# Four products of a constant in every step of TensorE's loop in the nodes stage

## The reference, cut to what matters

```
x = x + graph(layernorm(x)) + mix(layernorm(x))     # x1
u = layernorm(x)
logits = u @ gate_w + gate_b; idx = argmax(softmax(logits))
pos = running count of the rows of each expert; kept = pos < 977
y = relu(u_e @ w1[e] + b1[e]) @ w2[e] + b2[e]       # for the kept rows of expert e
x = x + y * prob
```

## Time and profile before

| what | value |
|---|---|
| median of three runs | 2139.8 us (2136.44 to 2140.73) |
| the profiled execution | 2139.9 us, span 2138.3 us |
| mean granted clock of TensorE | 0.787 of 2.4 GHz |
| nodes stage in the span | about 1544 to 1671 us |
| busy in the span | PE 1593.7, DVE 1387.2, POOL 1036.1, ACT 721.3 us |

### The profile page before, as it was taken

One profiled execution on the slowest core, in us unless ns is written; L12 is line 12 of the kernel. 1 busy time (PEld: TensorE's weight loads), 2 busy tenths in 40 slices (PEclk: granted clock), 3 DMA queues, 4 the chain that ended last, 5 costly groups with the idle time before them and its releaser, 6 DMA issues. The chain is left out here.

```text
span 2138.3 us, 26245 instructions
## 1 busy us (share of the span) xinstructions
PE 1593.7 (75%) x6551; PEld 889.5 (42%) x6551; DVE 1387.2 (65%) x4056; ACT 721.3 (34%) x2020; POOL 1036.1 (48%) x1021
## 2 busy tenths in 40 slices
PE   4666887677878777365555658888676699999997
PEld 3552332233333333022222224554365466666665
DVE  7568998789999998366656555555465144444444
ACT  3336997004877776000000001111064122222221
POOL 2001001777777777777777777777425111111111
PEclk9788999767999999555555557667555799999999
DMA  5117000333333333933333344444844422222200
GB/s 167 40 40 295 31 0 15 100 101 96 94 97 97 99 97 99 99 110 103 103 101 103 102 114 130 123 121 128 102 155 168 133 89 89 97 92 92 91 23 5
DMA packets 89183, 210.70 MB, mean 99 GB/s; under 512 B 20627, under 2 KB 49849, under 8 KB 86081
## 3 DMA queue, kind: packets, MB, share of 16 engines
q0 software_dynamic: 51888, 138.08, 24.8%
q1 hardware_dynamic: 35496, 70.56, 9.7%
q10 hardware_dynamic: 1680, 0.67, 0.2%
HBM read 163.98 MB, written 49.89 MB: 100 GB/s over the span
## 5 line engine op out<-in xcount | busy, mean ns | idle before, releaser
L902 DVE TENSOR_TENSOR XA<-XA,bank 128x257 f32 x880 | 369.0, 419 | 345.0 <-PE bank L657 319.5
L439 POOL DMA_INDIRECT G<-xn_parts,idx x440 | 443.0, 1007 | 277.7 <-DVE srcl L994 143.9
L439 POOL DMA_INDIRECT w<-xn_parts,idx x440 | 451.3, 1026 | 134.1 <-issue 134.1
L656 PE MATMUL bank<-G,S 128*128 128x257 f16 x440 | 154.8, 352 | 165.2 <-DMA G<-xn_parts,idx 140.4
L1582 POOL DMA_INDIRECT out<-ob,tok x64 | 66.6, 1040 | 401.7 <-DVE ob L1568 399.0
L656 PE MATMUL bank<-w,S 128*128 128x257 f16 x440 | 152.6, 347 | 138.8 <-DMA w<-xn_parts,idx 124.0
L529 ACT ACTIVATE LV<-LH,v 125x128 f16<-125x128 f16 x600 | 182.9, 388 | 189.5 <-DVE LH L1063 189.2
L1506 PE MATMUL bank<-w,ht 128*117 128x256 f32 (+1 forms) x1024 | 223.7, 379 | 0.0
L1495 PE MATMUL bank<-xt,w 128*128 128x468 f32 (+1 forms) x512 | 215.3, 579 | 0.8 <-ACT xt L1520 0.8
L1506 PEld LDWEIGHTS bank<-w,ht 128*117 128x117 f32 (+1 forms) x1024 | 188.8, 186 | 30.5 <-issue 0.4
L1530 ACT ACTIVATE ht<-bank,b1c 128x468 f32<-128x468 f32 (+1 forms) x128 | 85.7, 670 | 333.8 <-PE bank L1495 333.8
(11 more groups left out here) (225 smaller groups left out, 2542.9 us busy)
## 6 DMA issues: line engine op xcount, KB each, us to landing
w<-f SPq DMA_DIRECT2D x16, 1024.0 KB, 7.4
expert_rows<-G SPq DMA_DIRECT2D x7, 2048.0 KB, 21.3
xb<-expert_rows SPq DMA_DIRECT2D x8, 1028.0 KB, 11.4
xb<-expert_rows SPq DMA_DIRECT2D x8, 939.7 KB
G<-xn_parts,idx POOLq DMA_INDIRECT x440, 2.8
w<-xn_parts,idx POOLq DMA_INDIRECT x440, 2.8
XA<-x SPq DMA_DIRECT2D x6, 1024.0 KB, 5.7
xn_parts<-G POOLq DMA_DIRECT2D x12, 512.0 KB, 3.7
```

Source lines behind the costliest of these rows:

```text
L439: pool.indirect_dma_start(g[:, o:o + 2 * D], None, tab, bass.IndirectOffsetOnAxis(ap=idx[:, t:t + 1], axis=0)).then_inc(s_g[t % RING], 16)
L656: pe.matmul(psA[t % AR][:, 0:AGW], lhs, g[:, o + D:o + 2 * D + 1], start=True, stop=True)
L902: v.tensor_tensor(XA[:, ds(o, AGW)], XA[:, ds(o, AGW)], psA[t % AR][:, 0:AGW], ALU.add).then_inc(s_ev, 1)
```

## The change

At the head of each of the 66 steps of TensorE's loop in `nodes` it multiplies a constant (the tile of ones, read as 16-bit numbers) by itself four times, 128x128 by 128x256, into PSUM bank 0, which nobody reads. That is 264 products. In the first 49 steps a wait stands ahead of them: TensorE waits until DVE has finished x1 of block n. Nothing else changes.

```diff
@@ nodes
     PT, PD = 64, 128
+    FILL = 4
...
     @block.tensor
     def _(pe):
+        idle = ones[:, :].bitcast(F16)
         for n in range(STEPS):
+            if n < NB:
+                pe.wait_ge(s_x1, n + 1)
+            for _ in range(FILL):
+                pe.matmul(bank[0][:, 0:2 * P], idle[:, 0:P], idle[:, 0:2 * P], start=True, stop=True)
             m = blk(n, GATE)
```

## The result

| | before | after |
|---|---|---|
| median | 2139.45 us (2136.44 to 2140.73) | 2164.71 us (2155.68 to 2167.45) |
| ratio to before, with its 95% interval | | 1.0111 [1.0089, 1.0132] |
| the profiled execution | 2139.9 us | 2163.4 us, span 2161.8 us |
| mean granted clock | 0.787 | 0.800 |
| PE busy in the span | 1593.7 us, 6551 instructions | 1618.7 us, 6815 instructions |

The account below looks back on a forecast made before the run. The prediction took a ring of TensorE's transposes and ACT's copy and normalising, no engine full, to bound `nodes`. Terms -0.8 + 5.0 + 18.7 + 10.7 - 1.5 = +32.1 on 2139.9 gave 2172.0 us, range 2153 to 2179.

Parts of the forecast that it names:

- L8 to L15: `nodes`, line 1376 of step 8 to that of step 15: full clock, shorter steps, 0.8 us faster.
- L15 to L22: `nodes`, line 1376 of step 15 to step 22: a 19.85 us batch at clock 0.50, less 0.8; 5.0 us slower.
- L22 to L43: `nodes`, line 1376 of step 22 to step 43: three batches of 19.85 us against 13.62, 18.7 us slower.
- L43 to the last places: `nodes` tail, line 1376 of step 43 to the end of L1364: 44.3 us against 33.57, 10.7 us slower.
- hidden by POOL: End of `nodes`: POOL's last batch begins about 0.8 us after the places, before 2.26; saves 1.5 us.
- TensorE's own step at clock 0.50: Undisturbed steps of `nodes`: transposes 0.46, 0.83 to the next work, products 0.85; 2.14 us, more than the old 1.65.
- rival 2: `nodes`: the clock comes and goes, one or two of four batches at 1.00; 2152 to 2167 us, chance 0.22.
- rival 1: `nodes`: the full clock holds through the stage, batches of 15.03 us; about +3, 2143 us, chance 0.08.
- Rival 3: `nodes`: the clock never rises, the constant or too few products not lifting it; +37.6, 2177 us, chance 0.20.
- Rival 4: `nodes`, start of each step: full clock holds, wait costs nothing as line 1376 runs ahead; 2128 us, chance 0.03.
- Rival 5: `nodes`: the products pass beside everything or fall away, no difference; 2140 us, chance 0.02.
- one ring: `nodes`: the wait closes a loop through TensorE, ACT and DVE's line 1376; 19.85 us a batch at 0.50, against 13.62.

Follow-up runs that it names:

- the wait at the full clock: Against the changed kernel: products set by schedule (5, 11 or 9 a step, none in the tail), from step 9 the wait behind them; 2143.29 us, 1.0020 of before.

## Why the prediction was right, and where it was off

**The sum, term by term** (us, from the starts of line 1376 and the last places in the two traces):

| stretch | forecast | measured | how |
|---|---|---|---|
| L8 to L15 | -0.8 | -0.6 | 10.53 against 11.15 |
| L15 to L22 | +5.0 | +4.05 | 18.08 against 14.03 |
| L22 to L43 | +18.7 | +15.5 | 19.10 + 18.13 + 19.11 against 40.86 |
| L43 to the last places | +10.7 | +7.8 | 41.41 against 33.57 |
| hidden by POOL | -1.5 | -1.5 | 0.80 against 2.26 |
| sum | +32.1 | +25.3 | |

The mechanism held in each stretch, and each of the long ones was made too dear: by a fifth to a quarter up to L43, by over a third in the tail. The 0.3 us between the +25.3 of the sum and the 25.0 in the trace is the way from POOL's last batch to `experts`. **The term that was mis-sized is TensorE's own step at clock 0.50**, put at 2.14 us and measured at 1.95. I had added the transposes (0.46), the time from the logits to the next transposes (0.83) and the products (0.85) as if they followed each other; measured are 0.43 for transposes to logits, 0.71 for logits to products and 0.81 for products to transposes. The 0.83 of the earlier trace rows was read in the one step of a batch that has the prefix sums: the logits behind them take 0.98 us and not 0.86, and what follows starts 0.83 after them and not 0.71. The changed kernel has the same 0.83 there, though its next work is the products (they start at 1650.00):

```profile
1649.17 0.98 PE L1293 MATMUL bank<-gw,ut 128*128 128x8 f32 x4
```

So 0.12 us that belong to one step were put into every step. That is 0.12 of the 0.19, and 0.04 and 0.03 are in the other two. Three such steps in a batch are 3 x 0.19 = 0.57 of the 0.75 us by which a batch at 0.50 was too long (19.85 against 19.10). The other hops were good: 1.36 for line 1376 to the transposes (forecast 1.35), 3.21 from transposes to the exponential's reader (3.26), 1.47 to the prefix sums' reader (1.52), 3.50 to the next batch (3.54). Counted with their signs, they make the rest. In the tail the same error stands in every step to T57, which came 31.8 us after L43 (33.7 forecast); and from the last prefix sums to the last places, with the clock at 1.00, it took 3.82 us where 4.31 were put. One slip of the working, 4.87 for L1320 where its terms give 4.85, bears on nothing. And the square roots of steps 8 and 15 have no table load ahead of them (the trace before has its first in the stage at 1569.17, for the exponential), as the forecast took it for L15, and not as the kernel's description has it for all batches.

**Second, the clock.** Forecast: 1.00 from about 1552 to 1563, 0.50 after. The trace has 1.00 from 1550.3 for 13.7 us, to 1564.0, then 0.50 with returns at 1608.4 (3.4 us), 1659.6 (3.4) and 1673.2 (6.8). The first return made one batch 18.13 us where the others took 19.1, the last one helped in the tail. That is a small part of rival 2, and its price (up to 4.8 us a batch) fits the 1.0 us of so short a return. The median, 2164.71, lies in the band that rival 2 was given (2152 to 2167), but mostly not by way of the clock: of the 6.8 us between 32.1 and 25.3 the clock gave about 1.7 (an estimate: 1.0 in the batch of 18.13, 0.2 in the batch before L22, 0.5 behind the last prefix sums), the size of the step nearly all of the rest. That the range held owes something to the width that rival 2 had given it. The fall came in a stretch in which PE was busy for little more than half of the time: 2.20 of 4 us from 1560 to 1564, longest idle time 1.64 us, ended by the x1 of the boundary. The clock also fell without the wait (products alone: 0.57 over 70 us), so the wait isn't its only cause. The rule of the Trainium skill that I had weighed as rival 1 ("TensorE: Matmul & The Clock Gate", section "Why this matters for your kernels": no long idle gaps between bursts keep the full clock) does not hold for the changed kernel: from 1550.3 to 1564.0 no idle time of TensorE was over 1.64 us, and the clock fell. The trace before could have told: at 851.5, in the stretch of the earlier trace rows, the clock fell with no idle time above 1.68 us from 827 to 853. And with the wait at the full clock TensorE idled 1.84 or 1.85 us at each of four boundaries, and the clock fell behind two of them (at 1594.4 and 1608.0) and not behind the others. What decides it stays open.

**Rivals.** Rival 1's price was fair: the wait with the full clock costs 14.1 us a batch (I had 15.03 for products behind the wait; here they stood ahead of it, which spares 0.44 at each of three places and would give 13.7, but a plain step took 1.42 to 1.45 us and not 1.34, with transposes of 0.41 to 0.44 in place of 0.38) and makes the kernel 1.9 us longer in the trace, where I had some 3. The clock didn't hold, though, with four products in each step. Rival 3 was wrong for 128 partitions of the constant and right for one. Rival 4 fell at the place I named: x1 of the boundary step comes after TensorE could have started, in every batch. Rival 5 is excluded by the time.

**Of what I said the trace would show**, right were the order at the boundary (transposes after line 1376 and four products), TensorE without idle time in plain steps, ACT waiting longer for it (43.4 us against 27.0), and the unmoved way from the last scatter batch to `experts` (22.99 against 23.31 us). None of the signs that would have made me wrong appeared: batches at 0.50 took over 18 us, and the clock fell at the first boundary, if 2.5 us after L15 and not with it.

**One thing the forecast left out** is that the loss isn't a sum of the wait's and the products' parts. The working had both in one ring and so was right on the total, but a reader could not have told from it that the wait alone costs 11.0 us, the products alone 2.2, and that only swapping their order gives back 10.0 of the 25.0 (all by the traces).

## What to carry to other kernels

When a wait is put at the head of an engine's loop, look for the batch boundaries and ask which work used to run ahead of the signal: that is what becomes serial, whatever the steps between look like. Work that is there only for the clock was better ahead of a wait than behind it here, and best in the number that fills the engine's idle time: the same 264 products cost 25.0 us behind the wait, 15.0 ahead of it and 2.2 without it, and 351 placed by schedule, with the wait in the first nine steps alone, gave 8.3 us back. Add up an engine's step from distances between starts measured in the same kind of step: one taken behind the prefix sums was 0.12 us too long for all the others.

## What the runs showed of the hardware

- Filling TensorE with products of a constant that nobody reads raised the granted clock when they used all 128 partitions (1.00 after 1550.3 us in the changed kernel) and not when they used one (0.50 with PE busy for 10.00 of 10 us).
- Placed to fill the holes, they held 2.4 GHz for 88.7 us in a stage that had been at 1.2 GHz throughout, and made the ring of transposes and ACT faster, 13.62 to 12.17 us a batch: the two transposes on it took 0.44 us in place of 0.69, the plain step 1.40 in place of 1.65.
- Products of one partition between work on 128 cost more than products of 128: 2.23 against 1.95 us a step. Why wasn't tried apart.
- 28 such products (5.3 us) behind 24.08 us of idle time, ahead of the next stage, let its first transposes run at 2.4 GHz (1.09 against 1.97 us for eight) and made the stage 3.0 us shorter in the trace.
- The clock fell from 2.4 to 1.2 GHz at 1564.0 in the changed kernel with no idle time of TensorE above 1.64 us, and kept 2.4 GHz across two boundaries of 1.84 us in the kernel with the wait at the full clock.
